# Attention scores of the second graph layer taken from the normalised rows, an added mask, and a bias matmul over all partitions

## What is computed

```python
# second graph layer, X = layernorm(x)
H = X @ W_fc + b_fc
s_src = H @ w_att[:d]
s_dst = H @ w_att[d:]
scores = s_src[:, None] + s_dst[None, :] + b_att
scores = jnp.where(A > 0, scores, jnp.float32(NEG_INF))
alpha = jax.nn.softmax(scores, axis=1)
x = x + alpha @ H
# recurrent layer, gates i, g, o of step t (f reaches no output)
i_t = sigmoid(x_t @ U_i + b_i + h @ V_i)
g_t = tanh(x_t @ U_c + b_c + h @ V_c)
o_t = sigmoid(x_t @ U_o + b_o + h @ V_o)
c = h * c + i_t * g_t
h = o_t * tanh(c)
```

## Time and profile before

| | |
|---|---|
| median of 3 executions | 2936.88 us (2936.61 to 2938.2) |
| the profiled execution | 2939.59 us |
| its span, first to last instruction | 2937.8 us |
| PE busy | 2472.8 us (84%) |
| DVE busy | 1919.2 us (65%) |
| ACT busy | 1443.9 us (49%) |
| POOL busy | 171.9 us (6%) |
| mean granted TensorE clock | 0.978 |

### The profile page before, as it was taken

How to read it: one execution, slowest core, us unless ns; L and a number is a source line. 1 busy time by engine, 2 the same in 40 slices (tenths; PEclk the granted TensorE clock), 3 DMA queues, 4 the chain that set the end, 5 groups by cost and what they waited for, 6 DMA issues and landing times.

```text
span 2937.8 us, 79857 instructions
## 1 busy us (share of the span) xinstructions
PE 2472.8 (84%) x26334; PEld 1211.4 (41%) x26334; DVE 1919.2 (65%) x15110; ACT 1443.9 (49%) x8446; POOL 171.9 (6%) x130
## 2 busy tenths in 40 slices
PE   4989867888888888888888888888888888888887
PEld 4434422444444444444444444444444444444443
DVE  5457789666666666666666666666666666666666
ACT  5432123455555555555555555555555555555554
POOL 0540067000000000000000000000000000000000
PEclk8999978999999999999999999999999999999999
DMA  7010000000000000000000000000000000000000
GB/s 253 1 36 1 0 0 6 2 2 2 2 2 2 2 2 2 2 2 2 2 2 2 2 2 2 2 2 2 2 2 2 2 2 2 2 2 2 2 2 16
DMA packets 12877, 27.59 MB, mean 9 GB/s; under 512 B 1971, under 2 KB 9654, under 8 KB 10422
## 3 DMA queue, kind: packets, MB, share of 16 engines
q1 hardware_dynamic: 10406, 22.02, 2.2%
q10 hardware_dynamic: 2064, 0.55, 0.1%
HBM read 21.52 MB, written 1.05 MB: 8 GB/s over the span
## 4 chain that ended last, share of the span: by engine, by line
ACT 41%; PE 32%; DVE 16%; issue 9%; DMA 1%; POOL 0%; SPq 0%; DVEq 0%; POOLq 0%; ACTq 0%
ACT work L674 24%; PE psum L506 14%; DVE work L997 12%; ACT work L665 11%; ACT psum L667 5%; PE psum L510 5%; PE psum L419 4%; PE psum L360 2%; PE psum L477 2%; PE psum L371 1%; PE psum L485 1%; DMA work<-in_adj_dram 1%; DVE work L909 1%; DVE FT L946 1%; PE psum L399 1%
## 5 line engine op out<-in xcount | busy, mean ns | idle before, releaser
L477 PE MATMUL psum<-MASKT,identity_b 128*128 128x448 bf16 x6076 | 1480.9, 351 | 0.0
L506 PEld LDWEIGHTS psum<-work,MASK 128*128 128x128 f16 x12288 | 596.6, 96 | 1179.0 <-DVE work L997 1171.5
L506 PE MATMUL psum<-work,MASK 128*128 128x1 f16 x12288 | 774.0, 165 | 344.4 <-DVE work L997 343.7
L665 ACT ACTIVATE work<-psum 128x1 f32<-128x1 f32 x2048 | 351.2, 171 | 1128.8 <-PE psum L510 1128.8
L674 ACT ACTIVATE work<-psum,work 128x2 f32<-128x2 f32 x2048 | 721.7, 352 | 2.8 <-issue 2.8
L510 PE MATMUL psum<-work,MASK 128*128 128x1 f16 x6144 | 668.5, 168 | 0.0
L994 DVE TENSOR_SCALAR work<-work 128x1 f32<-128x1 f32 x2048 | 315.0, 154 | 495.7 <-ACT work L669 495.7
L997 DVE TENSOR_TENSOR_SCAN work<-work 128x3 f16<-128x3 f32 x2048 | 341.7, 167 | 294.0 <-ACT work L674 6.0
L477 PEld LDWEIGHTS psum<-MASKT,identity_b 128*128 128x128 bf16 x6076 | 436.8, 96 | 185.2 <-issue 2.9
L510 PEld LDWEIGHTS psum<-work,MASK 128*128 128x128 f16 x6144 | 493.1, 96 | 0.0
L1007 DVE SCALAR_TENSOR_TENSOR work<-psum,work 128x1 f32<-128x1 f32 x2048 | 433.3, 212 | 0.0
(11 more groups left out here) (144 smaller groups left out, 1100.9 us busy)
## 6 DMA issues: line engine op xcount, KB each, us to landing
work<-in_adj_dram SPq DMA_DIRECT2D x16, 1024.0 KB, 4.9
work<-in_L_ffn_Wd_dram SPq DMA_DIRECT2D x4, 512.0 KB, 6.1
out_dram<-work SPq DMA_DIRECT2D x4, 256.0 KB, 2.7
work<-in_L_ffn_bd_dram SPq DMA_DIRECT2D x1, 512.0 KB, 6.8
W<-in_L_ffn_W_dram ACTq DMA_DIRECT2D x1, 256.0 KB, 2.9
watt<-in_L_gnn_w_att_dram ACTq DMA_DIRECT2D x2, 64.0 KB, 7.0
work<-in_L_gnn_Wq_dram SPq DMA_DIRECT2D x1, 64.0 KB, 8.2
Wfc<-in_L_gnn_W_fc_dram ACTq DMA_DIRECT2D x1, 64.0 KB, 5.6
```

What stands on the lines that cost most here:

```text
L477: nc.tensor.matmul(bank(b)[:, HALF:CH], identity_b[:], MASKT[:, part % NGATE, 0:CH - HALF], start=False, stop=False, skip_group_check=True)
L506: nc.tensor.matmul(into, Vparts[:, gate, part, :], h_steps[:, q, 2:3], start=False, stop=False, skip_group_check=True)
L665: nc.scalar.activation(sig_i[:, q], bank(NGATE * k)[:, col:col + 1], ACT.Sigmoid, scale=1.0 / SCALE_V).then_inc(i_ready, 1)
```

## The change

It does five things.

1. `w_att` (128 x 2) holds W_fc times the two halves of the attention vector, `b_att` (128 x 2) the products with b_fc. VectorE forms them ahead of the feed-forward layer, and spreads the second column over 128 columns in `watt[:, 1, :]`.
2. TensorE forms the row s_dst chunk by chunk from FT and `watt[:, 1, :]`; ScalarE alternates the copy to FT with the copy to s_row, which adds the bias. The product with W_fc follows behind, and beside each tile a matmul with two columns (`w_att`) gives s_dst and s_src as columns in bank 6. Lines 268 to 270, 444 to 450 and 892 to 902 go.
3. The argument adds the mask in place of taking the minimum, so a row with no neighbour gets its mean by the ordinary sum. L784, L785, L939 and L953 go from this layer.
4. The bias matmul contracts over all 128 partitions: `bias_rows` is zero but for its first row. VectorE clears it after step 13 of the third chunk, and the loads of the recurrent weights wait for that.
5. The order on GpSimd and SyncE follows from it.

```diff
+            pe.wait_ge(w_ready, 1)
             for c in range(NCH):
                 pe.wait_ge(ft_copied, 2 * NCH + c + 1)
+                if c >= 2:
+                    pe.wait_ge(srow_copied, c - 1)
+                nc.tensor.matmul(bank(4 + c % 2), watt[:, 1, :], FT[:, c * CH:(c + 1) * CH],
+                                 start=True, stop=True).then_inc(srow_ready, 1)
+                if c < 2:
+                    transpose_rows(2, (c + 2,))
+            for c in range(NCH):
                 if c >= 2:
                     pe.wait_ge(h2_taken, c - 1)
                 for t in range(TPC):
                     i = TPC * c + t
                     last = nc.tensor.matmul(bank_rows(2 + c % 2)[:, t, :], FT[:, i * P:(i + 1) * P], Wfc[:],
                                             start=True, stop=True)
                 last.then_inc(h2_ready, 1)
-                if c < 2:
-                    transpose_rows(2, (c + 2,))
+                for t in range(TPC):
+                    i = TPC * c + t
+                    last = nc.tensor.matmul(bank(6)[:, 2 * i:2 * i + 2], FT[:, i * P:(i + 1) * P], w_att[:],
+                                            start=True, stop=True)
+            last.then_inc(scol_ready, 1)
             pe.wait_ge(h2_taken, NCH)
-
-            for c in range(NCH):
-                pe.wait_ge(sdiag_ready, c + 1)
-                nc.tensor.matmul(bank(4 + c), ones[:], dst_diag[:, c * TPC:(c + 1) * TPC, :].rearrange("p t d -> p (t d)"),
-                                 start=True, stop=True).then_inc(srow_ready, 1)
-            for t in range(NT):
-                last = nc.tensor.matmul(bank(0)[:, 0:P], ones[:], H2[:, t, :], start=t == 0, stop=t == NT - 1)
-            last.then_inc(mean_ready, 1)
-            pe.wait_ge(srow_copied, NCH)
...
-                nc.tensor.matmul(bank(NGATE * k + gate)[:, 0:HALF], gate_bias[:, gate, :], ones[0:1, 0:HALF],
+                nc.tensor.matmul(bank(NGATE * k + gate)[:, 0:HALF], bias_rows[:, gate, :], ones[:, 0:HALF],
                                  start=True, stop=False, skip_group_check=True)
...
-            copy_ft(2)
             for c in range(NCH):
+                act.wait_ge(ft_transposed, 2 * NCH + c + 1)
+                nc.scalar.copy(FT[:, c * CH:(c + 1) * CH], bank(c % 2)).then_inc(ft_copied, 1)
                 act.wait_ge(srow_ready, c + 1)
-                nc.scalar.copy(s_row[:, c * CH:(c + 1) * CH], bank(4 + c)).then_inc(srow_copied, 1)
+                nc.scalar.activation(s_row[:, c * CH:(c + 1) * CH], bank(4 + c % 2), ACT.Identity,
+                                     bias=b_att[:, 1:2]).then_inc(srow_copied, 1)
...
+            dve.wait_ge(gat_loaded, 80)
+            link = Chain(dve, w_chain)
+            for w in range(2):
+                link.step(v.tensor_tensor_reduce(YB[:, 0, :], Wfc[:], watt[:, w, :], 1.0, 0.0, ALU.mult, ALU.add,
+                                                 w_att[:, w:w + 1]))
+                link.step(v.tensor_tensor_reduce(YB[:, 0, :], bfc[:], watt[:, w, :], 1.0, 0.0, ALU.mult, ALU.add,
+                                                 b_att[:, w:w + 1]))
+            v.tensor_copy(watt[:, 1, :], w_att[:, 1:2].to_broadcast([P, P])).then_inc(w_ready, 1)
...
-            dve.wait_ge(h2_taken, NCH)
-            chain.step(v.tensor_tensor(product[1], H2, watt[:, 1, :].unsqueeze(1).to_broadcast([P, NT, P]), ALU.mult))
-            chain.step(v.tensor_reduce(s_dst[:], product[1], AX.X, ALU.add))
...
+            dve.wait_ge(scol_ready, 1)
+            s_cols = bank(6)[:, 0:2 * NT].rearrange("p (t w) -> p w t", w=2)
+            chain.step(v.tensor_scalar(s_dst[:], s_cols[:, 1, :], b_att[:, 1:2], None, ALU.add))
+            chain.step(v.tensor_scalar(s_src[:], s_cols[:, 0, :], b_att[:, 0:1], batt[:], ALU.add, ALU.add))
...
+                if c + 2 == NCH and j == 13:
+                    dve.wait_ge(mask_free, NT)
+                    v.memset(bias_rows, 0.0).then_inc(bias_zeroed, 1)
...
-                                       ALU.add, ALU.min).then_inc(s["arg_ready"], 1)
+                                       ALU.add, ALU.add).then_inc(s["arg_ready"], 1)
...
-                link = invert_sums(s, c, steps)
-
-                for t in range(TPC):
-                    last = v.scalar_tensor_tensor(x_row(c, t), mean, empty[:, t:t + 1], x_row(c, t), ALU.mult, ALU.add)
-                link.step(last)
-                assert link.count == steps
+                link = Chain(dve, s["chain"], c * steps)
+                dve.wait_ge(s["den_ready"], c + 2)
+                link.step(v.reciprocal(rden[:], bank(5)[:, 0:TPC]))
```

More of the change, by code:

```diff
@@ L87, in build_program @@
         Wfc = sb("Wfc", [P, P])
+        w_att = sb("w_att", [P, 2])
+        b_att = sb("b_att", [P, 2])
         bfc = sb("bfc", [P, P])
@@ L138, in build_program @@
         s_row = region(N, N)
-        product = [region(2 * N, N, "p (t d) -> p t d", t=NT), region(RING, N, "p (t d) -> p t d", t=NT)]
-        dst_diag = region(RING + N, N, "p (t d) -> p t d", t=NT)
         scratch = region(2 * N, N // 2).bitcast(BF16)
-        mean = region(2 * N + N // 2, P)
         diag = region(3 * N, CH, "p (t d) -> p t d", t=TPC)
@@ L159, in build_program @@
         V = mask_words[:, NGATE * P:2 * NGATE * P].rearrange("p (g d) -> p g d", g=NGATE)
+        bias_rows = mask_words[:, 2 * NGATE * P:3 * NGATE * P].rearrange("p (g d) -> p g d", g=NGATE)
         gate_bias = mask_words[0:1, 2 * NGATE * P:3 * NGATE * P].rearrange("p (g d) -> p g d", g=NGATE)
@@ L198, in build_program @@
         h2_ready, h2_taken = sem("h2_ready"), sem("h2_taken")
[L199 to L202, removed]
+        w_chain, w_ready, scol_ready = sem("w_chain"), sem("w_ready"), sem("scol_ready")
+        srow_ready, srow_copied, mask_free = sem("srow_ready"), sem("srow_copied"), sem("mask_free")
+        bias_zeroed, rec_start = sem("bias_zeroed"), sem("rec_start")
         i_summed, g_summed, o_summed = sem("i_summed"), sem("g_summed"), sem("o_summed")
@@ L227, in _ @@
             sp.dma_start(bd, a["L0_ffn_bd"].rearrange("(o e) c -> o e c", o=1).to_broadcast([P, NE, P])).then_inc(wd_loaded, 16)
-            sp.wait_ge(mask_free, NT)
+            sp.wait_ge(bias_zeroed, 1)
             for k, name in enumerate(("i", "c", "o")):
@@ L266, in _ @@
             sum_exps(g[0])
-            pool.wait_ge(h2_taken, NCH)
-            pool.wait_ge(gat_loaded, 80)
-            pool.tensor_tensor(product[0], H2, watt[:, 0, :].unsqueeze(1).to_broadcast([P, NT, P]), ALU.mult).then_inc(src_product, 1)
             sum_exps(g[1])
@@ L429, in _ @@
             transpose_rows(2, range(2))
-            pe.wait_ge(gat_loaded, 80)
+            pe.wait_ge(w_ready, 1)
             for c in range(NCH):
                 pe.wait_ge(ft_copied, 2 * NCH + c + 1)
+                if c >= 2:
[5 more added lines that the diff above has]
+            for c in range(NCH):
                 if c >= 2:
@@ L886, in _ @@
             layernorm(())
-            dve.wait_ge(gat_loaded, 80)
             for c in range(NCH):
@@ L891, in _ @@
                                 bfc[:].unsqueeze(1).to_broadcast([P, TPC, P]), ALU.add).then_inc(h2_taken, 1)
-            dve.wait_ge(h2_taken, NCH)
-            chain.step(v.tensor_tensor(product[1], H2, watt[:, 1, :].unsqueeze(1).to_broadcast([P, NT, P]), ALU.mult))
-            chain.step(v.tensor_reduce(s_dst[:], product[1], AX.X, ALU.add))
-            for c in range(NCH):
-                here = slice(c * TPC, (c + 1) * TPC)
-                v.tensor_tensor(dst_diag[:, here, :], identity[:].unsqueeze(1).to_broadcast([P, TPC, P]),
-                                s_dst[:, here].unsqueeze(2).to_broadcast([P, TPC, P]), ALU.mult).then_inc(sdiag_ready, 1)
-            dve.wait_ge(src_product, 1)
-            chain.step(v.tensor_reduce(s_src[:], product[0], AX.X, ALU.add))
-            chain.step(v.tensor_scalar(s_src[:], s_src[:], batt[:], None, ALU.add))
+            dve.wait_ge(scol_ready, 1)
+            s_cols = bank(6)[:, 0:2 * NT].rearrange("p (t w) -> p w t", w=2)
+            chain.step(v.tensor_scalar(s_dst[:], s_cols[:, 1, :], b_att[:, 1:2], None, ALU.add))
+            chain.step(v.tensor_scalar(s_src[:], s_cols[:, 0, :], b_att[:, 0:1], batt[:], ALU.add, ALU.add))
             dve.wait_ge(srow_copied, NCH)
@@ L937, in _ @@
                 largest(t)
-            dve.wait_ge(mean_ready, 1)
-            chain.step(v.tensor_scalar(mean, bank(0)[:, 0:P], 1.0 / N, None, ALU.mult))
             shifts(0)
@@ L946, in mask_score_1 @@
                 v.scalar_tensor_tensor(arg[j % NRING], bank(c), s_dst[:, j:j + 1], MASKT[:, j, c * CH:(c + 1) * CH],
-                                       ALU.add, ALU.min).then_inc(s["arg_ready"], 1)
+                                       ALU.add, ALU.add).then_inc(s["arg_ready"], 1)
             def weigh_sums_1(s, c, steps):
-                link = invert_sums(s, c, steps)
-                for t in range(TPC):
```

(10 more changed lines are left out.)

## The result

The changed kernel took 2918.69 us (median of 4 executions, 2916.99 to 2919.74) against 2937.54 us (2936.61 to 2938.34): a ratio of 0.9936, 95% interval 0.9923 to 0.9948. The profiled execution's span is 2917.4 us, 20.4 less than that of before.

A forecast was written before the change was run, and what follows sets the result against it. Bound: a chain of latencies, mostly in the recurrence, with no engine there at its limit. Gains 8.6 + 0.5 + 3.5 + 8.8 = 21.4 us take the profiled 2939.59 to 2918.2, median 2915.5; range 2908 to 2925.5.

The forecast's parts named there:

- Bias matmul: Recurrence: a one-partition matmul lets the array empty before and after itself; 128 partitions save 93 x 0.092 = 8.6 us.
- The rival that put the gap on the start of a bank set: Recurrence: the gap before L485 is not due to the partitions, so the bias term is nil; 2924.6 us, chance 12%.
- The stretch ahead of step 0: First three bias matmuls, before the recurrence: same gaps on a path also waiting for transposes; 0 to 1 us, taken 0.5.
- Score stage: Up to the first maximum: 15.1 us removed, alternating copies and score matmuls added; gain 3.2 us, plus 0.3 for L939.
- high throughout: Score stage: with TensorE's clock at the higher level all along, the first L909 starts at 379.2.
- Attention, chunk 1: Second graph layer: without L953 at most 5.1 us to gain, GpSimd needs 27.7, boundary stays a TensorE chain; 2.5 us.
- Chunk 2: Attention: 28.80 us now, GpSimd needs 25.8, idle GpSimd 0.55 and 2.55 us closes in part; gain 2.5 us.
- Chunk 3: Attention: 21.1 us now, 18.8 needed; VectorE starts splitting V earlier, so the last L778 follows the additions; 2.2 us.
- Close: End of the attention: L953's 1.14 us and two steps of 0.2 go; gain 1.6 us.
- VectorE as the bound: Attention and scores: VectorE gets back all its work, 12.1 and 5.0 us; 2910.7 us, chance 15%.
- that attention and scores give little: GpSimd's operand lock and TensorE's lower level in the score stage leave 4.5 and 0 us; 2923.3 us, chance 15%.
- TensorE at the lower level all along: Scores and attention: TensorE becomes the bound at its lower clock, chunks 32.2 us; slower, 2943 us, chance 3%.

The follow-up runs named there:

- shift_early: Changed kernel with TensorE's shift row of the next chunk issued before the matmul of step 13 instead of step 14: 2911.71 us, ratio 0.9916.
- fill: Changed kernel with discarded matmuls on TensorE during the first four maxima and after each attention matmul of the second graph layer: 2911.18 us.
- copies_ahead: Changed kernel with ScalarE copying the next transposed chunk before it evacuates the previous score chunk: 2913.45 us, one execution.
- mean_psum: Kernel before with the mean of H2 kept in PSUM instead of SBUF for L953: 2934.07 us, ratio 0.9982.
- the second set: Changed kernel as it is, executed again: 2915.1 us against 2938.76, ratio 0.9918.
- attention_only: Kernel before with part 3 alone (mask added; L784, L785, L939, L953 and the mean's matmuls gone): 2926.42 us, ratio 0.996.
- scores_only: Kernel before with parts 1 and 2 alone (scores by TensorE; minimum, L953, mean's matmuls and one-partition bias kept): 2934.32 us, ratio 0.9984.
- best_all: Changed kernel with earlier shift row, copies ahead, one 130-column matmul per tile for H2 and scores, and discarded matmuls: 2903.9 us, ratio 0.9878.

## Why the prediction was right

2918.7 came where 2915.5 was forecast, inside the range, and the three mechanisms were those of the text. Point by point:

- **Bias matmul:** forecast 8.6 in the recurrence, 8.99 in the profile, of which 0.4 are the two slow first steps of before, whose clock was low; steps 56, 58 and 60 gave 8.58. The rival that put the gap on the start of a bank set is out: the changed kernel still starts its bank sets, with a period of 1.17. The stretch ahead of step 0 gave 1.82 for 0.5; the runs put about 0.9 on the bias matmuls and 1.0 on the clock level.
- **Score stage:** 3.2 forecast, 4.64 measured. The order of the chain was right, and its terms nearly so: 1.14 us for a score chunk at the higher level where I had 0.85, 1.2 for ScalarE between them where I had 1.5, 0.25 and 0.20 for a tile of H2 and a pair of columns. The term that was mis-sized is the stretch at the lower level, 1.5 us, that I put in because TensorE is idle half the time; the lower level did not return there. Without the 2.9 us by which this trace began late, the first L909 started at 379.3, and the bound "high throughout" was 379.2. (The other bound should be -2.8 and not -3.1: the 0.3 of L939 is missing in it.)
- **Attention, chunk 1:** 2.5 forecast, 5.06 measured. The floor of 27.7 by GpSimd's additions was met, 27.76. The step that failed is the one followed behind it: the boundary. I took it to stay a chain over TensorE. GpSimd's idle time there fell from 6.57 to 0.81 us, which is more than the whole gain; its additions took 26.95, 0.7 more than with their gaps before. In the changed kernel the shift row took 1.02 us at the higher level, where one at the lower takes 1.72:

```profile
447.38 1.02 PE L454 MATMUL psum<-work,ones 128*128 128x512 f32 x2
```

- **Chunk 2:** 2.5 forecast, 0.89 measured, for the same step the other way round: there the lower level fell on the boundary (idle time 3.02 for 2.55), and shift_early and fill both take the missing 2 us out. With the level the other way about, in copies_ahead, the same chunks gained 3.40 and 2.95. The two errors cancel, 5.0 forecast for both chunks and 5.95 measured; that is luck in the parts, while the bound below them, 27.7 and 25.8, was right. (I also named one gap of 0.55 us in this chunk; there were five, 2.3 us together.)
- **Chunk 3:** 2.2 forecast, 1.58 measured. The additions took 19.0 us where I had 18.8, and I had the last L778 follow them at once. As L777 it came 0.5 us after them (they end at 501.61), because VectorE's splitting of V now stands beside GpSimd's last additions, and two of its operations grow to the length of one. L970 here took 0.36 before as L974:

```profile
499.18 1.30 DVE L970 TENSOR_SCALAR MASK<-MASK 128x384 f16<-128x384 f32 x1
500.52 1.30 DVE L971 TENSOR_SCALAR MASK<-MASK 1x384 f32<-1x384 f32 x1
501.85 0.36 DVE L972 TENSOR_SCALAR MASK<-MASK 128x384 f32<-128x384 f32 x1
502.12 0.69 DVE L777 TENSOR_TENSOR work<-work 128x512 f32<-128x512 f32 x1
```

- **Close:** 1.6 forecast, 0.75 measured. I asked what goes and not what is late next. L953 had hidden TensorE's transposes back (L345, now L341), and VectorE waits 0.84 us for them:

```profile
505.80 1.12 DVE L798 SCALAR_TENSOR_TENSOR X<-psum,rden,X 128x128 f32<-128x128 f32 x4 [0.84 <-PE psum L341]
```

  In both closes TensorE summed over partitions at the lower level (VectorE waits 1.96 us for it). Where it did so at the higher one (1.15 us), the gain is 1.0: 5.67 us with L953 (mean_psum), 4.67 without (shift_early).

- **Median:** the first trace started its second graph layer 2.9 us late, by chance, and its set of executions lies 3.2 above the forecast; the second set, at 0.9918, is 23.7 us below before, 2.3 beyond it.
- **The rivals:** VectorE as the bound is out by attention_only (8.3 us, not 12), that attention and scores give little by the same 8.3 and the 4.45 of scores_only, and TensorE at the lower level all along by the granted clock of 0.76 to 0.96.
- **The signs:** step 56 and the bias load came as said. The chunks behind the first were to take about 30, 26.5 and 19 us and took 27.8, 27.9 and 19.5: the first two did not come as said.

Not settled: why chunk 0 takes 29.7 to 29.9 us in some traces and 30.5 in others (in the longer ones its additions take 27.0 us with 3.50 idle behind them, in the others 29.0 with 0.80, so one of the maxima falls into the idle time), and why every second block of the recurrence has one step of 1.40 us, in all kernels alike.

## What to carry to other kernels

Look for rows of two instructions of the same size where one has idle time in front and the other has none, and ask what differs in their shape: here it was the number of partitions, and the added zeros cost nothing that these runs show. When an engine is freed of waits for another one, count what that other one needs for itself; that is the floor. Chunk 1 met it to 0.1 us, chunk 2 only once its boundary was mended, and chunk 3 stayed 0.7 above it. And when a step is taken off a chain, name what it had hidden at each of its places: at the close of the last chunk that cost half of the gain.

## What the runs showed that I had not expected

- A matmul over 64 partitions between matmuls over 128 costs as much as one over a single partition (0.09 us a step and 0.37 us of waiting for its load), one over 96 costs nothing.
- Where TensorE's clock fell went with which chunk's boundary was long. Chunks 1 and 2 of the same code took 27.8 and 27.9 us, or 29.4 and 25.9 (copies_ahead), as the level fell, and 27.8 and 25.8 with the level held by discarded matmuls, which cost 0.4 us in chunk 3 and 0.5 in best_all. The boundary behind chunk 2 is the only one where a run shows the clock to be the cause.
- VectorE operations with a single tensor input in SBUF (L970, 0.36 us alone) also grow to 1.30 us beside GpSimd's additions, not only those with two; with the additions over, L972 took 0.36 again.
